# A macaron block on one core: the attention part written out without loops

## The reference, cut to what matters

```python
x = x + 0.5 * ffn(layernorm(x))
x = x + attention(layernorm(x))
x = x + 0.5 * ffn(layernorm(x))
```

```python
logits = einsum('bnqhd,bnkhd->bnhqk', qb, concat(k_left, k_own, k_right, side_k)) + bias
m = max(logits.max(), 0)
probs = exp(logits - m) / (exp(logits - m).sum() + exp(-m))
y = einsum('bnhqk,bnkhd->bnqhd', probs, concat(v_left, v_own, v_right, side_v))
out = einsum('blhk,hkd->bld', y, Wo)
```

## Time and profile before

| | us |
|---|---|
| median of 3 runs (lowest and highest) | 2498.21 (2495.73 to 2502.98) |
| the profiled execution, and its span | 2508.59, 2506.5 |
| busy in the span: PE, ACT | 2198.1, 2140.6 |
| busy in the span: DVE, POOL | 1893.7, 1638.5 |

### The profile page before, as it was taken

How to read it: one execution, slowest core, us unless ns; L and a number is a source line. 1 busy time by engine, 2 the same in 40 slices (tenths; PEclk the granted TensorE clock), 3 DMA queues, 4 the chain that set the end, 5 groups by cost and what they waited for, 6 DMA issues and landing times. The chain is left out here.

```text
span 2506.5 us, 98603 instructions
## 1 busy us (share of the span) xinstructions
PE 2198.1 (88%) x34394; PEld 1693.7 (68%) x34394; DVE 1893.7 (76%) x4448; ACT 2140.6 (85%) x4422; POOL 1638.5 (65%) x1453
## 2 busy tenths in 40 slices
PE   1888885899899889999988998998899999979998
PEld 0555553677777767777776777777677777746666
DVE  6789986687687767777776876877677777758876
ACT  2988882899899879989987998998799899869998
POOL 1677775577677657767765776776576677647765
PEclk9999996999999999999999999999999999989999
DMA  5100000999999999999999999999999999911001
GB/s 186 49 0 0 0 1 18 144 160 159 146 162 162 160 141 160 160 148 163 163 159 140 161 162 149 162 158 156 144 162 156 158 158 160 157 32 34 33 25 42
DMA packets 1111389, 300.24 MB, mean 120 GB/s; under 512 B 1091440, under 2 KB 1109872, under 8 KB 1110896
## 3 DMA queue, kind: packets, MB, share of 16 engines
q1 hardware_dynamic: 1110896, 294.00, 77.9%
HBM read 14.68 MB, written 8.39 MB: 9 GB/s over the span
## 5 line engine op out<-in xcount | busy, mean ns | idle before, releaser
L987 POOL TENSOR_TENSOR probs_split<-probs,probs_split 128x512 f16<-128x512 f32 (+1 forms) x1026 | 1156.6, 1127 | 578.8 <-ACT probs_split L1267 577.2
L1313 DVE CUSTOM_DVE_ANT_0 score_ps<-score_ps,mask,neg_qk_scale 128x512 f32<-128x512 f32 (+1 forms) x1028 | 750.0, 730 | 337.1 <-PE score_ps L1091 319.8
L1267 ACT ACTIVATE probs_split<-probs 128x512 f16<-128x512 f32 (+1 forms) x1026 | 632.3, 616 | 133.9 <-ACT probs L1252 93.8
L1252 ACT ACTIVATE probs<-score_ps,minus_max 128x512 f32<-128x512 f32 (+1 forms) x1027 | 683.4, 665 | 54.9 <-DVE minus_max L1313 49.4
L1109 PE MATMUL y_ps<-v_parts,probsT 128*128 128x64 f16 x11922 | 520.1, 194 | 96.7 <-DMA probsT<-probs_split 93.3
L1109 PEld LDWEIGHTS y_ps<-v_parts,probsT 128*128 128x128 f16 x11922 | 455.8, 98 | 215.1 <-DMA probsT<-probs_split 157.2
L1088 PE MATMUL score_ps<-k_parts,q_parts 64*128 64x128 f16 (+1 forms) x4524 | 420.7, 235 | 30.7 <-issue 25.1
L1091 PE MATMUL score_ps<-k_parts,q_parts 64*128 64x128 f16 (+1 forms) x4524 | 420.7, 235 | 0.0
L1088 PEld LDWEIGHTS score_ps<-k_parts,q_parts 64*128 64x128 f16 x4524 | 279.2, 94 | 73.9 <-issue 35.8
L1091 PEld LDWEIGHTS score_ps<-k_parts,q_parts 64*128 64x128 f16 x4524 | 279.2, 94 | 0.0
L1020 PE MATMUL item_ps<-b_xT,wk_split 128*128 128x128 f16 x3168 | 223.0, 221 | 13.3 <-DVE b_xT L1305 6.5
(11 more groups left out here) (173 smaller groups left out, 3969.2 us busy)
## 6 DMA issues: line engine op xcount, KB each, us to landing
probsT<-probs_split SPq DMA_TRANSPOSE x1033, 4.1
out_x<-x_resident SPq DMA_DIRECT2D x16, 512.0 KB, 2.9
x_resident<-in_L_attn_x SPq DMA_DIRECT2D x14, 512.0 KB, 4.3
raw_up<-in_L_ffn_w_up SPq DMA_DIRECT2D x1, 1024.0 KB, 5.7
raw_down<-in_L_ffn_w_down SPq DMA_DIRECT2D x1, 1024.0 KB, 7.6
raw_q<-in_L_attn_Wq SPq DMA_DIRECT2D x1, 1024.0 KB, 9.5
raw_k<-in_L_attn_Wk SPq DMA_DIRECT2D x1, 1024.0 KB, 11.5
raw_v<-in_L_attn_Wv SPq DMA_DIRECT2D x1, 1024.0 KB, 13.2
```

Of the source, the lines that this page charges most:

```text
L987: nc.gpsimd.tensor_tensor(parts_of[v % NPARTS][:, LO, cols], probs[v % NBUF][:, cols], parts_of[v % NPARTS][:, HI, cols], ALU.subtract).th ...
L1252: nc.scalar.activation(probs[v % NBUF][:, cols], score_ps[v % NBUF][:, cols], ACT.Exp, bias=bias[:, j % 2, h:h + 1], scale=-1.0, accum_out ...
L1267: nc.scalar.activation(parts_of[v % NPARTS][:, HI, cols], probs[v % NBUF][:, cols], ACT.Copy).then_inc(phi_done.sem, 1)
L1313: nc.vector.tensor_tensor_reduce(out=score_ps[v % NBUF][:, cols], in0=score_ps[v % NBUF][:, cols], in1=w.mask[:, cols], scale=w.neg_qk_sca ...
```

## The change

The three loops of `batches` become plain loops of the program that writes the code, so all 16 rounds stand there one after the other, with numbers in place of registers. The calls of `separate` in the attention and its semaphore go. Which instruction does what, and in which order, stays as it was, and so do all the numbers that waits compare with. The same calls in `ffn_phase` stay.

```diff
-        passed = sem("b_passed")
         block = ctx.enter_context(nc.Block())
-
-        def separate(eng):
-
-            eng.sem_inc(passed, 1)
...
         def batches(eng, body):
-            with eng.Fori(0, BATCH) as b:
-                body(At(b, 0), b)
-                with eng.Fori(1, ROUNDS - 1) as i:
+            for b in range(BATCH):
+                for i in range(ROUNDS):
                     body(At(b, i), b)
-                body(At(b, ROUNDS - 1), b)
...
                 plo_done.wait(sp, at.heads + v)
-                separate(sp)
                 pv_done.wait(sp, at.heads + v - NBUF)
-                separate(sp)
                 sp.dma_start_transpose(pt[v % NBUF][:], parts_of[v % NPARTS][:].rearrange("p s n -> p (s n)")
...
                 max_done.wait(act, at.heads + v)
                 cols = columns(place_of(at, v))
-                separate(act)
                 plo_done.wait(act, at.heads + v - NBUF)
-                separate(act)
                 nc.scalar.activation(probs[v % NBUF][:, cols], score_ps[v % NBUF][:, cols], ACT.Exp, bias=bias[:, j % 2, h:h + 1],
...
                 exp_done.wait(act, at.heads + v)
-                separate(act)
                 act.wait_ge(turned[v % NPARTS], turn_count(at, v - NPARTS))
-                separate(act)
                 nc.scalar.activation(parts_of[v % NPARTS][:, HI, cols], probs[v % NBUF][:, cols],
...
                 scores_done.wait(dve, at.heads + v)
-                separate(dve)
                 nc.vector.tensor_tensor_reduce(out=score_ps[v % NBUF][:, cols], in0=score_ps[v % NBUF][:, cols],
...
             def mean_variance():
                 step_done()
-                separate(dve)
                 mark(nc.vector.bn_aggr(mv[:], stats[:]))
```

## The result

| | us |
|---|---|
| the changed kernel, median of 4 runs (lowest and highest) | 2383.35 (2376.26 to 2387.8) |
| the kernel before, median of 4 runs | 2497.86 |
| ratio, 95% interval | 0.9536, 0.9508 to 0.9564 |
| the profiled execution, its span | 2383.82, 2382.1 |

It is 114.5 us faster, where 86 were forecast (2412, range 2368 to 2460). The direction and the place were right, three terms of the sum were not. The measured time lies at the forecast's halfway mark to rival B (2382).

The account below looks back on a forecast made before the run. The prediction took ACT to set the attention's pace, with SP's transpose queue nearly as full. Loops 34, ACT's gap 36 and waits for DVE 16 sum to 86 us off 2498, giving 2412 us, range 2368 to 2460.

Parts of the forecast that it names:

- rival B: Attention: ACT's gap closes to 0.03 us and all DVE waits away from batch edges go; 146 us, 2352 us; chance 0.14.
- Loops, 34 us: Attention loops: written out, the seven jumps and ACT's 34 us of "issue" waits go, without new stalls in straight code.
- Rival C: Attention: straight code stalls when drawn from memory, a late PE packet costing 3.93 us; slower, 2667 us; chance 0.05.
- ACT's gap, 36 us: ACT's high-part copy waiting for its own exponential: one of two instructions goes, 0.08 us at 451 places, 36 us.
- SP, nothing by itself: SP's transpose issues: 0.13 us less per head, mean interval 1.64 to 1.51 us, so ACT's gain is not given back.
- Waits for DVE, 16 us less: ACT's exponential waiting for DVE's row maxima, 49.4 us: half of the 31 us away from batch edges goes, 16 us.
- Rival A, only the jumps go: DMA engines set the transposes' pace, SP's issue grows by what its waits lose; 34 us gained, 2464 us; chance 0.12.
- The excess of the issues: SP's mean interval over its best, 0.15 us a head: put down to long issues and code packets; it stays.

Follow-up runs that it names:

- kernel with an outer loop: The kernel before, each batch's four rounds written out, the loop over batches, its register arithmetic and all separating instructions kept: 2491.22 us, ratio 0.995.
- the last experiment: The changed kernel with feed-forward loops also written out, their separating instructions dropped, a fifth transposed-probabilities bank, and SP's bank wait only at even heads: 2367.64 us, ratio 0.9459.

## Why the prediction was right where it was, and wrong where it was

*Loops, 34 us: right in the profile.* ACT's 34.1 us of "issue" are gone, the rounds are even but for the batches' extra items, and no stop of several microseconds appears in straight code; PE's "issue" waits before its score loads fell from 33.6 to 10.4 us. Rival C did not happen. But the term covered only what a jump stops. The kernel with an outer loop and the one with SP alone in it show a second cost of loops, the arithmetic in SP's queue, for which the forecast had no term.

*ACT's gap, 36 us: the size failed, in its premise.* "The first wait still needs an instruction of its own and the second can ride on the copy" is the wrong way round. The wait for the exponential is written first and rides, and the gap closed to 0.03 us: 80 us of idle time, rival B's 81. That is the first half of rival B; its second half, the waits for DVE, did not come, and the time stopped halfway. In the two runs that put parts of the gap back, 77 us of it are worth 28 us of time, and 28 us are worth none. So "on the path since ACT sets the pace" failed too: it held only until SP became as slow.

*SP, nothing by itself: the step that failed most.* The working found SP in arrears by 1.6 us and at ACT's pace of 1.64 us, and then used that only as a condition ("Had SP kept 1.64 us, it would"). Tested, that condition is the larger part of the gain: with SP nearly as before (three jumps in place of seven) and all else changed, the ratio is 0.9889 against 0.9517. "SP falls behind no more" did not come true either: it issues 0.88 us behind POOL, and 88% of the issues are over 0.3 us late. The forecast interval was about right (1.36 at best, measured 1.38), and the mean less so (1.51 forecast, 1.57 measured), because its excess did not stay at 0.15 us; issues grew as they came closer together.

*Waits for DVE, 16 us less: wrong.* They stayed at 49.0 us. The runs show what they are: the place where ACT feels SP's limit. They fall when ACT is slowed (16.7 us), rise when SP is (75.1, 106.8), and fall when the DMA engines are relieved (26.2).

*Rival A, only the jumps go: wrong as a whole, right in its mechanism.* "SP's issue grows by what its waits lose" happens, but for a part: 0.06 us of the mean for 0.16 us less between (0.250 to 0.092, medians), from the outer-loop kernel to the changed one. In the last experiment it is all of it.

*The sum* came within 29 us in part by luck, because errors offset: the gap's closing was twice as wide as I took it and worth a third, the waits for DVE gave nothing, and SP's relief, counted at nothing, was worth more than any other term.

*The excess of the issues.* The forecast put it down to long issues and to code packets on the same DMA engines, without a test. Nothing here tests it by an edit, but the traces speak for it. In the kernel before, 545 of the 1025 issues have an instruction packet that starts between 1 us ahead of the issue and its end. They take 1.54 us in the mean, the others 1.24, and of the 295 issues over 1.3 us 267 are among them. With halved transposes all 244 long issues are among such, and none of the 594 others is long. Less code did not make the excess smaller, though: what the issues take beyond their median sums to 170 us before and 171 us after.

What stays open: by what way an instruction packet would lengthen an issue, and what holds the interval at 1.39 us when fewer instructions lie between two issues. That halved transposes bring it down says that the bytes have a part in it; which part of the way they load was not tried.

## What to carry to other kernels

When two engines keep the same pace, count the relief of both or of none: here a relief of ACT alone or of SP alone gave some 19 us each and both together 45. A queue that only issues DMAs has no busy time on the page; look at the distance of its issues, and count every addition and semaphore instruction between two of them as time of the kernel. Before a wait is merged with another, draw the ring it closes: a ring of three banks that takes 5.2 us to go round made a kernel 3.9% slower that had one instruction less at every second head.

## What the runs showed of the hardware

- Of two waits in front of one instruction, the one written first came to ride on it (0.03 us from release to start) and the second got an instruction of its own (0.10 us if it is the late one; 0.21 us with two separate instructions).
- The same transposing DMA issue took 1.232 us (median) when 0.25 us lay between two of them, 1.252 us at 0.18 and 1.291 us at 0.09. Below that nothing was gained: at 0.10 and 0.04 in turn it took 1.283 and 1.341 us.
- Between the end of one issue and the start of the next lay 0.04 us (median) with no instruction between them, 0.09 us with one semaphore instruction, 0.18 us with two, and 0.25 us with two and a register addition.
- A jump back over a long body stopped ACT for 3.9 to 6.1 us; straight code of the same work stopped no compute engine for more than 0.4 us (PE's weight loads), and ACT not at all.
- Halving a transpose's bytes left its issue nearly as long (1.291 to 1.220 us) and brought the landing from 4.1 to 2.6 us.
